# Two graph layers on one core: first pass in a new order, second projection as three products of split halves

## What is computed

```
x = _layernorm(x + _L0_gnn_ref(x, adj, L0_gnn_w))     # A = adj + I; deg = sum(A, axis=1)
                                                      # A_hat = A * deg^-1/2 [rows] * deg^-1/2 [columns]
                                                      # elu((A_hat @ x) @ w)
x = _layernorm(x + _L1_gnn_ref(x, adj, L1_gnn_W, L1_gnn_b))
                                                      # relu((adj @ x) @ W.T + b)
```

## Time and profile before

| | us |
|---|---|
| median of 3 runs | 887.83 |
| profiled execution | 887.87 |
| its span, first to last instruction | 885.7 |
| PE busy | 793.4 (90%), 3532 instructions |
| PEld busy | 653.1 (74%) |
| DVE busy | 740.4 (84%) |
| ACT busy | 511.9 (58%) |
| POOL busy | 189.3 (21%) |
| granted TensorE clock, mean | 0.968 |

### The profile page before, as it was taken

The page is one execution under the profiler, slowest core; times in us unless marked ns, Lnnn a source line. Parts: engine busy times, 40 slices in busy tenths (PEclk is TensorE's granted clock), DMA queues, the critical chain, the costliest instruction groups (busy, mean ns, idle before and its releaser), DMA issues.

```text
span 885.7 us, 10783 instructions
## 1 busy us (share of the span) xinstructions
PE 793.4 (90%) x3532; PEld 653.1 (74%) x3532; DVE 740.4 (84%) x611; ACT 511.9 (58%) x1132; POOL 189.3 (21%) x181
## 2 busy tenths in 40 slices
PE   0447959599999999899999999999999999999996
PEld 0335748477878888688888888888888888888884
DVE  2368878798989998698998999898989898888963
ACT  2254646465866564368876755756653765455351
POOL 0003341341344520012221101111210322022021
PEclk9967969899999999999999999999999999999998
DMA  9999987697799999879999977989896898997500
GB/s 273 306 307 292 215 156 174 163 248 186 168 268 283 186 225 215 189 185 213 225 211 210 243 207 197 193 218 194 205 245 197 182 249 183 220 219 178 130 24 25
DMA packets 183590, 181.71 MB, mean 205 GB/s; under 512 B 6768, under 2 KB 183536, under 8 KB 183536
## 3 DMA queue, kind: packets, MB, share of 16 engines
q1 hardware_dynamic: 94704, 93.21, 45.7%
q10 hardware_dynamic: 88832, 87.83, 42.6%
HBM read 176.82 MB, written 4.19 MB: 204 GB/s over the span
## 4 chain that ended last, share of the span: by engine, by line
PE 58%; DVE 1%; issue 0%; ACT 0%; POOLq 0%; POOL 0%; DVEq 0%; ACTq 0%
PE acc L972 18%; PE acc L974 18%; PE acc L973 18%; PE proj L931 3%; PE proj L929 1%; PE acc L952 0%; DVE v_lo L684 0%; DVE stats L837 0%; DVE raw L831 0%; PE acc L1004 0%; ACT v_hi L477 0%; ACT normed L610 0%; POOLq L173 0%; DVE mean_var L842 0%; POOL rstd L445 0%
## 5 line engine op out<-in xcount | busy, mean ns | idle before, releaser
L972 PE MATMUL acc<-a_hi,v_hi 128*128 128x512 f32 x1024 | 408.4, 399 | 43.2 <-DVE a_lo L643 27.6
L457 ACT ACTIVATE a_hi<-turned 128x1024 fp32r<-128x1024 f32 x256 | 264.5, 1058 | 277.6 <-PE acc L974 131.3
L973 PE MATMUL acc<-a_lo,v_hi 128*128 128x512 f32 x1024 | 403.4, 394 | 0.0
L974 PE MATMUL acc<-a_hi,v_lo 128*128 128x512 f32 x1024 | 403.1, 394 | 0.0
L643 DVE TENSOR_TENSOR a_lo<-turned,a_hi 128x1024 fp32r<-128x1024 f32 x256 | 313.1, 1258 | 42.8 <-ACT a_hi L457 32.4
L626 DVE STREAM_TRANSPOSE turned<-raw 128x2048 f32<-128x2048 f32 x122 | 280.0, 2302 | 8.5 <-DMA raw<-in_adj_dram 2.4
L972 PEld LDWEIGHTS acc<-a_hi,v_hi 128*128 128x128 f32 x1024 | 195.4, 191 | 87.3 <-issue 30.3
L974 PEld LDWEIGHTS acc<-a_hi,v_lo 128*128 128x128 f32 x1024 | 195.1, 191 | 41.4
L973 PEld LDWEIGHTS acc<-a_lo,v_hi 128*128 128x128 f32 x1024 | 195.3, 191 | 39.9
L467 ACT ACTIVATE acc<-raw 128x256 f32<-128x256 f32 x198 | 73.0, 368 | 23.0 <-DMA raw<-in_adj_dram 21.6
L418 POOL TENSOR_TENSOR raw<-raw,x_row 128x1024 f32<-128x1024 f32 x8 | 22.6, 2830 | 179.7 <-ACT raw L513 179.7
(11 more groups left out here) (69 smaller groups left out, 413.2 us busy)
## 6 DMA issues: line engine op xcount, KB each, us to landing
raw<-in_adj_dram SPq DMA_DIRECT2D x154, 512.0 KB, 9.5
raw<-in_adj_dram ACTq DMA_DIRECT2D x154, 512.0 KB, 10.0
x_row<-in_x_dram SPq DMA_DIRECT2D x64, 128.0 KB, 6.7
out_dram<-normed ACTq DMA_DIRECT2D x28, 128.0 KB, 3.2
held<-in_adj_dram ACTq DMA_DIRECT2D x4, 512.0 KB, 12.7
held<-in_adj_dram SPq DMA_DIRECT2D x4, 512.0 KB, 12.8
partial<-in_adj_dram ACTq DMA_DIRECT2D x2, 512.0 KB, 17.0
partial<-in_adj_dram SPq DMA_DIRECT2D x2, 512.0 KB, 18.5
```

The costliest lines, as they stand in the source:

```text
L457: nc.scalar.activation(a_hi[u % 2][:, part, :], turned[u % 2][:, part, :], ACT.Copy).then_inc(s_hi, 1)
L972: pe.matmul(dst, v_hi[:, k, ch], a_hi[u % 2][:, t, :], start=begin, stop=False)
L973: pe.matmul(dst, v_hi[:, k, ch], a_lo[u % 2][:, t, :], start=False, stop=False)
L974: ins = pe.matmul(dst, v_lo[:, k, ch], a_hi[u % 2][:, t, :], start=False, stop=end)
```

## The change

The first pass gets another order. At the last block of rows 0 to 3 (`closing`), ACT issues its loads first, then makes the high halves of the next unit (`ahead_of`, the first unit of this block or else of the next one) and then y; DVE transposes that unit ahead of the degree sum, and does its low half and `y_low` right behind `deg_row`. PE turns x one block earlier and projects it one block earlier. SP loads x of rows 1 to 3 behind a row's first block. ACT's loads stand at the start of a block (`loads_first`) where the buffer has long been free. y's halves count by tile (`s_y`, `s_yhi`), so that a unit can start on the first tile. The identity is added to all four diagonals by one instruction. y of row 7 is made one block earlier, at the start of pass B.

In the second layer the aggregate and the transposed weights are each split into a high half (ACT, f32r) and a low half (DVE); the projection is 24 products of 128x128 by 128x256 in f32r, one unit later than before (`PROJECT_AT + 1`), and likewise for the last row, tile by tile. The halves lie where the third buffer and `w_sb`, `wt_sb` were.

```diff
     for n in range(AHEAD, len(chunks)):
-        loads_at[max(n - AHEAD, -1 if before[n] is None else done_at[before[n]])].append(n)
+        freed = -1 if before[n] is None else done_at[before[n]]
+        if n < FIRST_B and freed < n - AHEAD:
+            loads_first[n - AHEAD].append(n)
+        else:
+            loads_at[max(n - AHEAD, freed)].append(n)
...
+    ahead_of = {n: (visits[n] or visits[n + 1])[0] for n in range(PANELS - 1, PANELS * FAST, PANELS)}
...
@@ SP
-                    n = PANELS * m + (1 if m < FAST else 2)
+                    n = PANELS * m + (1 if m == 0 else 0 if m < FAST else 2)
...
@@ ACT
+            def split_wt():
+                act.wait_ge(s_wt, 1)
+                act.wait_ge(s_xw, GROUPS)
+                nc.scalar.activation(wt_hi[:], wt_sb[:], ACT.Copy).then_inc(s_whi, 1)
+            def agg_high(a):
+                i = order_of[a]
+                act.wait_ge(s_agg, i + 1)
+                nc.scalar.activation(agg_hi[:], agg, ACT.Copy).then_inc(s_ahi, 1)
...
-                if n == PANELS - 1:
+                load_others(loads_first[n])
+                if closing:
+                    hi_and_later(ahead_of[n])
                     make_y(row)
                 for u in visits[n]:
-                    hi_and_later(u)
+                    if u not in ahead_of.values():
+                        hi_and_later(u)
...
-                load_others(n)
-                if summed_first and n > PANELS:
-                    make_y(row)
-                if at == (2 if row < FAST else 3):
+                load_others(loads_at[n])
+                if at == (1 if row < FAST else 3):
                     keep_xt(row)
...
-                    if u == visits[n][0] and n == FIRST_B + Y_AT:
+                    if u == visits[n][0] and n == FIRST_B + 1:
                         make_y(GROUPS - 1)
+                        split_wt()
...
+                    for a in ended(u, AGG_AT, rows_done):
+                        if accs[a][2] == 1:
+                            agg_high(a)
...
             for t in range(GT):
                 act.wait_ge(s_used, halves_of(U - 1, 1))
                 nc.scalar.activation(*last_agg(1, t), ACT.Copy).then_inc(s_aggl1, 1)
+                if t:
+                    high_last(t - 1)
+            high_last(GT - 1)
...
@@ DVE
-                    for t in range(GT):
-                        diag = turned[u % 2][:, t, :].rearrange("p (q t r) -> p t q r", q=STRIPES, r=B32)[:, t]
-                        ins = nc.vector.tensor_tensor(diag, diag, ident[:].rearrange("p (q r) -> p q r", r=B32), ALU.add)
-                    ins.then_inc(s_turn, 1)
+                    diag = diagonal_of(turned[u % 2])
+                    nc.vector.tensor_tensor(diag, diag, ident4, ALU.add).then_inc(s_turn, 1)
...
+            def agg_low(a):
+                dve.wait_ge(s_ahi, order_of[a] - GROUPS + 1)
+                nc.vector.tensor_tensor(agg_lo[:], agg, agg_hi[:].bitcast(F32), ALU.subtract).then_inc(s_alo, 1)
...
+                if closing:
+                    raw_loaded(dve, n)
+                    deg_part(n)
+                    turn_and_low(ahead_of[n])
+                    turned_through[0] = ahead_of[n] + 1
+                    if n >= POOL_FROM:
+                        deg_of_pool(n)
                     deg_sum(row)
+                    deg_row(row)
+                    low_and_later(ahead_of[n])
+                    y_low(row)
...
-                if n == FIRST_B + 3:
+                if n == FIRST_B + 2:
                     y_low(GROUPS - 1)
+                    dve.wait_ge(s_whi, 1)
+                    nc.vector.tensor_tensor(wt_lo[:], wt_sb[:], wt_hi[:].bitcast(F32), ALU.subtract).then_inc(s_wlo, 1)
...
             for t in range(GT):
                 agg_last(t)
+                if t:
+                    low_last(t - 1)
+            low_last(GT - 1)
...
@@ PE
+            def by_wt(dst, h, t, begin):
+                own = slice(P * t, P * (t + 1))
+                pe.matmul(dst, agg_hi[:, h, own], wt_hi[:, h, :], start=begin, stop=False)
+                pe.matmul(dst, agg_hi[:, h, own], wt_lo[:, h, :], start=False, stop=False)
+                return pe.matmul(dst, agg_lo[:, h, own], wt_hi[:, h, :], start=False, stop=h == CH - 1)
...
                 for t in range(GT):
+                    if layer == 0:
+                        pe.wait_ge(s_y, GT * col + t + 1)
...
+                if row < FAST and at == 1:
+                    turn_x(row)
                 if row < FAST and at == 2:
-                    turn_x(row)
+                    project_x(row)
                 if row < FAST and at == 3:
-                    project_x(row)
                     fold_degrees(row)
...
                 for a in ended(u, PROJECT_AT, rows_done):
-                    project(a)
+                    if accs[a][2] == 0:
+                        project(a)
+                for a in ended(u, PROJECT_AT + 1, rows_done):
+                    if accs[a][2] == 1:
+                        project(a)
```

More of the change, by code:

```diff
@@ L246, in gnn_two_layers @@
         s_xw = sem("xw_ready")
+        s_yhi = sem("y_hi_ready")
+        s_y = sem("y_ready")
         s_vhi = sem("v_hi_ready")
@@ L322, in last_agg, with diagonal_of @@
             return dst, src
+        def diagonal_of(tile):
+            whole = tile[:]
+            return bass.AP(whole.tensor, whole.offset, [list(whole.ap[0]), [GN + B32, GT], [P, STRIPES], [1, B32]])
         block = ctx.enter_context(nc.Block())
@@ L419, in _ @@
                 else:
-                    pool.wait_ge(s_v, GROUPS + row + 1)
+                    pool.wait_ge(s_v, row + 1)
                     if i > GROUPS:
@@ L549, in normalise, with load_others @@
                         act.dma_start(nodes_part(out, row, q), normed[B32 * q:B32 * (q + 1), :, :]).then_inc(s_out, 16)
-            def load_others(n):
-                for m in loads_at[n]:
+            def split_wt():
[6 more added lines that the diff above has]
+                nc.scalar.activation(agg_hi[:], agg, ACT.Copy).then_inc(s_ahi, 1)
+            def load_others(some):
+                for m in some:
                     if before[m] is not None:
@@ L601, in _, with high_last @@
                         normalise(a)
+            def high_last(t):
+                act.wait_ge(s_aggl, t + 1)
+                act.wait_ge(s_aggl1, t + 1)
+                own = slice(P * t, P * (t + 1))
+                nc.scalar.activation(agg_hi[:, :, own], agg[:, :, own], ACT.Copy).then_inc(s_ahil, 1)
             act.wait_ge(s_proj, order_of[LAST])
@@ L662, in deg_sum @@
                 if PANELS * row >= POOL_FROM:
-                    deg_of_pool(PANELS * row + PANELS - 1)
                     dve.wait_ge(s_degp, PANELS * (row + 1) - POOL_FROM)
@@ L679, in y_low @@
             def y_low(row):
-                dve.wait_ge(s_vhi, row + 1)
                 for t in range(GT):
                     k = tiles(row).start + 2 * t
-                    ins = nc.vector.scalar_tensor_tensor(out=v_lo[:, k, :], in0=proj[:, t, :],
-                                                         scalar=dinv[:, GT * row + t:GT * row + t + 1],
-                                                         in1=v_hi[:, k, :].bitcast(F32), op0=ALU.mult, op1=ALU.subtract)
-                ins.then_inc(s_v, 1)
+                    dve.wait_ge(s_yhi, 2 * row + t // 2 + 1)
+                    nc.vector.scalar_tensor_tensor(out=v_lo[:, k, :], in0=proj[:, t, :],
+                                                   scalar=dinv[:, GT * row + t:GT * row + t + 1],
+                                                   in1=v_hi[:, k, :].bitcast(F32), op0=ALU.mult,
+                                                   op1=ALU.subtract).then_inc(s_y, 1)
             def add_partial(a):
@@ L755, in low_and_later @@
                     aggregate(a)
+                for a in ended(u, AGG_AT + 1, rows_done):
+                    if accs[a][2] == 1:
+                        agg_low(a)
                 for a in ended(u, RESIDUAL_AT, rows_done):
@@ L802, in _ @@
                         turn_and_low(u)
+                        turned_through[0] = u + 1
+                if not closing:
                     raw_loaded(dve, n)
                     deg_part(n)
-                    if n == 1:
-                        keep_wt()
                     if row > FAST and at == 0:
                         deg_row(row - 1)
-                    if visits[n]:
-                        low_and_later(visits[n][-1])
-                    if at == PANELS - 1:
-                        deg_sum(row)
+                if n == 1:
+                    keep_wt()
+                if visits[n]:
+                    low_and_later(visits[n][-1])
+                if at == PANELS - 1 and not closing:
+                    deg_of_pool(n)
+                    deg_sum(row)
             for n in range(FIRST_B, len(chunks)):
-                if n == FIRST_B + 3:
+                if n == FIRST_B + 2:
```

(9 more changed lines are left out.)

69 lines of the change are left out of this document (41 added, 28 removed).

## The result

The changed kernel takes 882.07 us (median of 4 runs, 880.91 to 882.69) where the kernel before takes 887.52 beside it: a ratio of 0.9938, with a 95% interval of 0.9918 to 0.9957. That is 5.5 us faster, where 25.4 were forecast, and outside the range of 855 to 877. The profiled execution spans 880.9 us, 4.8 less than before.

The account below looks back on a forecast made before the run. TensorE bounds it after 364.5 us; before about 200 us it waits for others. First pass -17.9, last row of y -6.0, projection -4.0, second layer's work +1.1, end +1.4: -25.4 from 887.87 gives 862.5 us, range 855 to 877.

Parts of the forecast that it names:

- ACT has room: Second layer: ACT's added copy per row fits, DVE has little room; together +1.1 us, ends 0 and 5.
- First pass: Closings of rows 1 to 3 overlap with the next unit's work, so PE waits less: -17.9 us by unit (3,3).
- I leave the landing where it is: Row 1, first pass: last block lands unchanged, DVE has its degrees at 68.1, PE starts at 72.6, not 76.10.
- The credit of 1.0 us for a shorter slow start: Row 2's first unit, first pass: idle falls from 10.99 to 3.0 us, so less slow-clock time, 1.0 us saved.
- 12.2 us forecast to be left: First pass, row 2: lead remaining after DVE limits for a moment behind the row's first unit, 12.2 us.
- Last row of y: Before 364.50: y's halves made a block earlier remove PE's 4.30 us wait and 1.7 slow start, -6.0 us.
- Projection: Second layer: 24 f32r products of 0.12 us, 2.88 for 3.45 us, seven times: -4.0 us, ends -5.8 and +14.5.
- Both rivals on the pace of 256 columns: Second-layer projection: products no faster than 512 columns, 881.0 us, chance 0.10; or loads not hidden, 895 us, chance 0.05.
- End: Last row: more ACT copies before DVE's last subtraction, residual 3.0 us behind the first copies instead of 1.6: +1.4 us.
- The rival with loads that do not hide: Second-layer projection: load and stream add to 0.306 us a product, 7.3 a projection, +27 us: 895 us, chance 0.05.
- Waits for a_lo in every row of the third pass: Sign of being wrong: PE waiting for DVE's low half in each third-pass row; small waits near its first rows were expected.
- a shift of 18 us at 175 that shrinks by 360: Sign of being wrong: the first pass's lead of 18 us at 175 us is partly lost by 360 us.

Follow-up runs that it names:

- e3: Changed kernel with ACT's high half of the aggregate one unit later, behind that unit's high half and ahead of moments and normalising: 867.19 us, ratio 0.977.
- e12: Changed kernel with ACT's high half of the aggregate kept in its slot but placed last, behind moments and normalising: 867.16 us, ratio 0.9744.
- e4: Changed kernel without DVE's seven aggregate subtractions, the third product reading the high half again: 879.73 us, ratio 0.9915.
- e6: e3 with the third pass's two shortest rows, 7 and 6, projected in full f32 as before the change: 863.3 us, ratio 0.9727.
- e9: e6 with x of rows 1 to 3 back behind the second block of its row on SP's queue: 865.54 us, ratio 0.9753.
- e10: e6 with ACT's half of the loads back behind its own sums, as in the kernel before: 864.42 us, ratio 0.9742.
- e1: Changed kernel's earlier passes only, second layer projected in full f32 one unit earlier as in the kernel before: 867.82 us, ratio 0.9762.
- e8: e6 with the last row (row 0) in full f32 as well: 863.39 us.
- e2: Kernel before with only the second layer's split projection added, on the old first pass: 901.87 us, ratio 1.0162.
- e11: e6 with the identity added to a diagonal unit in four instructions instead of one: 865.06 us, ratio 0.9754.

## Why the prediction failed, step by step

**The step that failed** is "ACT has room": the second layer's added work at +1.1, with ends of 0 and 5. It counted busy time and DVE's load, and took the copy on ACT as 1.2 us on an engine 58% busy. By the stage of units 92 to 113 it cost 19.6 us. e3 and e12 show 15 of them as the knot of ACT's wait for DVE and DVE's wait for ACT, e4 4.0 as DVE's subtraction within that knot, and e6 that what e3 left goes when the two shortest rows are projected as before. The prediction looked for the tight place in DVE's order alone, and named nothing that stands behind the wait which the change put on ACT: behind `agg_high` stood normalising or moments, and for normalising waited DVE's residual (unit 100), for the high half behind them DVE's low half (units 104 and 109). What PE's idle time costs in clock was not in the sum either: 6.8 of the 19.6. That ACT comes to a slot earlier than DVE could be read before: DVE waits for ACT's high half of each unit, so ACT's slot ends when DVE's begins, and whatever ACT asks of DVE in the same slot comes a transposition and a split later. DVE's own share (4.0) was inside the ends of 0 to 5.

**First pass:** -14.95 for -17.9 at unit 24, but that is nearer than the working was. The forecast had its -17.9 at unit (3,3), number 12, and there the gain was 12.0 (162.43 against 174.43). The other 3.0 came behind it, where the sum had nothing (only its low end did), and are luck: after the wait before 188.54, as long as the one in the kernel before, the unit took 5.58 us and not 7.16, at a granted clock of 1.00 against 0.76; and a wait of 1.49 us for row 5's fold was gone.

Row 1's first unit started at 74.39, not 72.6, because its last block landed 1.5 us later: "I leave the landing where it is" failed. DVE's degrees of that block, before and after:

```profile
65.24 2.82 DVE L650 TENSOR_REDUCE deg_parts<-raw 128x10 f32<-128x2560 f32 x1 [3.20 <-DMA raw<-in_adj_dram]
```
```profile
66.78 2.82 DVE L705 TENSOR_REDUCE deg_parts<-raw 128x10 f32<-128x2560 f32 x1 [3.23 <-DMA raw<-in_adj_dram]
```

That is more than the spread: 65.24 and 65.36 in the two traces with the old first pass, 66.30 to 66.78 in the nine with the new one. Neither of the two parts that move transfers explains it (e9 and e10 land later still, at 67.97 and 67.34), so its cause stays open. Row 2's fold was 2.6 us later than forecast (111.76 for 109.2), most of it that inheritance, and dinv took 1.99 us in place of 1.04, as the timeline of POOL and DVE shows. The trace of the kernel before could have warned of it: beside a split its dinv took 1.95 us three times, the first in row 4 (first line):

```profile
225.99 1.95 POOL L398 TENSOR_TENSOR dinv<-deg,minus_half 128x4 f32<-128x4 f32 x1 [19.39 <-DVE deg L677]
```
```profile
112.31 1.99 POOL L425 TENSOR_TENSOR dinv<-deg,minus_half 128x4 f32<-128x4 f32 x1 [12.98 <-DVE deg L731]
114.38 0.24 POOL L427 TENSOR_SCALAR ndinv<-dinv 128x4 f32<-128x4 f32 x1
```
```profile
79.20 0.69 DVE L689 TENSOR_TENSOR turned<-turned,ident 128x512 f32<-128x512 f32 x1
...
112.07 0.16 DVE L731 TENSOR_SCALAR deg<-acc 128x4 f32<-128x4 f32 x1 [2.86 <-PE acc L965]
112.18 2.36 DVE L698 TENSOR_TENSOR a_lo<-turned,a_hi 128x1024 fp32r<-128x1024 f32 x2
115.53 1.66 DVE L738 SCALAR_TENSOR_TENSOR v_lo<-proj,dinv,v_hi 128x256 fp32r<-128x256 f32 x4 [0.99 <-ACT v_hi L504]
```

The low half that now runs under cover of fold and dinv is also what dinv ran beside. With both, unit 6 started at 116.07 for 112.4. The credit of 1.0 us for a shorter slow start behind it did not come: the first product took 0.79 us, as before (0.77), and of the 12.2 us forecast to be left 7.5 were there at the next unit (125.13 against 132.67). The one-piece diagonal took 0.69 for 0.55. The mechanism, closings overlapped with the next unit's transposition, was right: e1 alone gives 20 us with the last row of y.

**Last row of y:** -6.0 forecast. Units 24 to 42 took 6.75 less, and the wait before 364.50 is gone: right.

**Projection:** 0.12 us a product forecast, 0.120 measured; 0.57 us a row forecast, and two rows between units 113 and 127 save 1.13: right. Both rivals on the pace of 256 columns fall. Here loads recorded with 0.19 us followed each other every 0.12 us on the whole array. The Trainium skill, "TensorE: Matmul & The Clock Gate", Part 3, lets a load overlap with running products only where the row group differs, in its list of what overlaps; the measurement decides against that sentence, for 256 columns as for 512. The paragraph above that list also lets a load into a background weight buffer go ahead of running products; no row here shows which buffer a load goes to, but the pitch agrees with it.

**End:** +1.4 forecast, +0.65 between the two kernels and 1.1 between e8 and e6: right in kind, and 0.3 to 0.75 us too large. The first residual came 2.8 us behind the first copies (868.48 to 871.28), where 3.0 was forecast.

The rival with loads that do not hide was the only case on the slower side, and the wrong one; e2 shows that the second part alone was slower, by a mechanism that no rival named. "Waits for a_lo in every row of the third pass" was the sign given for being wrong, and came in part: five such waits, 12.7 us in all. The other sign, a shift of 18 us at 175 that shrinks by 360, did not come: the shift was 12.0 us at 162.43 and grew.

## What to carry to other kernels

Before a step is put on an engine that has room, name what stands behind it in that engine's order and who waits for that: where the engine that it waits for also waits for the work behind it, the two delays add up, however idle the engine is. Ask an engine only for what is a slot old, or make the asking the last thing in the slot: both moves were worth 15 us here, though in the second the engine still waited 23.8 us. Where rows follow each other closely, add no work to the engine that is full there, even if the step pays in the long rows: leaving two rows as they were gave another 3 us (130.15 for 133.12).

An effect of half a microsecond has to be read where identical code repeats: here the first pass spread over 3 us between traces of the same code, while units 92 to 113 took 130.13 to 130.16 in five traces (e6 and e8 to e11).

## What the runs showed of the hardware

A 1.22-us subtraction on DVE can take almost three times that, beside an addition of POOL (changed kernel, DVE and POOL):

```profile
716.86 3.42 DVE L785 TENSOR_TENSOR agg_lo<-raw,agg_hi 128x1024 fp32r<-128x1024 f32 x1
```
```profile
715.82 3.38 POOL L451 TENSOR_TENSOR x_row<-v_hi,v_lo 128x1024 f32<-128x1024 f32 x1
```

POOL ends at 719.20, and DVE 1.08 us later, about one undisturbed subtraction. The low half of unit 99 above shows the same: POOL's addition runs from 671.76 to 674.16, and the first half of the low half, begun at 672.67, is recorded until 675.25. The other way round, POOL's 3.38 us, where 2.40 is usual, began beside a low half of DVE that ended at 716.94. The Trainium skill, "SBUF — State Buffer", section "SBUF: two separate sides", says that the port pair of the two engines goes whole to whichever operation starts first, for an operation of DVE with two SBUF inputs against one of POOL that reads SBUF; these rows agree.

The small dinv agrees in one direction only. Begun 0.13 us behind the first half of a split, it took 1.99 us and ended 0.90 us behind that half (113.40), where 1.04 is its undisturbed time. But the second half, which ran beside it, took its usual 1.22 us. In row 1 dinv began first (72.62, 1.05 us), and the split begun 0.39 us behind it was not held either (1.23). So for an operation on 128x4 elements the rows do not show that DVE is kept out until it ends.

A wait of PE costs more than its length. Behind the wait of 2.44 us in e3 the next 7.20 us ran at a granted clock of 0.76, and unit 100 took 10.05 us in place of 8.3.
